# Rounded GELU values of a gated feed-forward block: a second GELU of ScalarE out of PSUM in place of VectorE copies of the first

## The chip, the cores and the metric

The kernel runs on one core of one Trainium2 chip. The metric is the device time of one execution in microseconds (us). Before the change it is 815.6 us, the median of three runs (814.63 to 817.16).

## The reference

A network of two layers is applied to 4 sequences of 1024 tokens of width 128. Each layer is an attention-like mixer and a feed-forward block, each with a residual sum and a layer norm behind it. The change lies in the last feed-forward block, the gated one, with its hidden width of 512:

```python
h = jax.nn.silu(_tlin(x, w1_w, w1_s)) * _tlin(x, w2_w, w2_s)
h = jax.nn.gelu(_tlin(h, h1_w, h1_s), approximate=False)
h = jax.nn.gelu(_tlin(h, h2_w, h2_s), approximate=False)
return _tlin(h, w3_w, w3_s)          # _tlin(x, w, s) = einsum('bsi,oi->bso', x, w) * s
```

The other three parts are a delta-rule attention over chunks of 32 tokens, a mixture of 8 experts (the two best count for each token; all eight are computed here), and a linear recurrence over time (LRU).

## The kernel before

The tokens go through in 8 tiles of 512 columns (4 sequences by 128 tokens), with the features on the partitions. Every large product is made of three float32r products, high by low, low by high and high by high (`mm3`), so each activation is wanted as a high part rounded to float32r and a low part, the difference of the value and its high part.

A software pipeline runs four tiles at a time. Its order is written out by hand and is the same on every engine (`schedule`). Two stages alternate. `dense(m, a, f)` runs the eight experts of tile m, with the delta rule of tile a between them, and at its start the output product of the gated block of tile f. `tails(f, m, a, l)` runs the gated block of tile f (f from 0 to 6), with the recurrence and norms of tile m and the end of attention, router and gates of tile a between its products. Tiles f = 2 to 4 are turns of a hardware loop, f = 0, 1, 5 and 6 are written out. `drain(6, 7)` does the last tile's gated block alone.

The order of `tails` on TensorE is: the gate and up products `glu(f, 0..3)`; `hidden(f, 0, O_H1)` (output blocks 0 and 1 of the first inner layer, into banks 4 and 5); the attention product and `lru_gates(m)`; `hidden(f, 2, O_H1)` (blocks 2 and 3, banks 6 and 7); the second inner layer's blocks 0 and 1 over input chunks 0 and 1; `mean_product`, `router`; the same blocks over input chunks 2 and 3; `var_product`; blocks 2 and 3; `gate_turn(a)`; and then, at the end of the stage, a wait for all four GELUs of the second layer (semaphore `h2_act`), since the next stage writes the banks that they read. In `tails(6, 7, None, 5)` the wait is left out and the drain has its own. TensorE runs its queue in order, so what stands behind that wait is the whole next `dense`.

A block of an inner layer goes through three engines: ScalarE applies GELU out of PSUM into `hf[:, o % 2]` (`gelu`, L1171, counted by `h1_act` or `h2_act`); VectorE copies that into the float32r tile `fbh` (first layer) or `fah` (second) (`hi`, L1888; L1954 in the drain; counted by `h1_hi`, `h2_hi`); GpSimd, called POOL in the profile, subtracts the two into `fbl` or `fal` (L1396, L1404; counted by `fb_ready`, `f2_ready`). The products wait for the last of these. On ScalarE the order of the stage is: four SiLU, norms, `gelu1(0)`, `gelu1(1)`, `lru_tanh` (L1036, L1038), decay and root of the recurrence, attention norm, `gelu1(2)`, `gelu1(3)`, the square of norm 3 (L1001), `gelu2(0)`, `gelu2(1)`, `gate_tanh` (L1057), the logarithm and exponential of norm 3 (table load L1240), `gelu2(2)`, `gelu2(3)`. GELU has its own table, so it is loaded before the first GELU of a group (ACT_TABLE_LOAD at L1171). In the experts a high part comes already from a second GELU of ScalarE (L1139, L1145).

Of the kernel before, what the change touches and what calls it, by code (L numbers as in the profile page):

```python
# [10 lines left out]
ACT = mybir.ActivationFunctionType  # L11
# [15 lines left out]
FC = FF // 128  # L27
# [20 lines left out]
def build(nc, io):  # L48
    ctx = ExitStack()
    with ctx:  # L50
# [25 lines left out]
        vec = sb("vec", [128, N_VEC])  # L76
# [142 lines left out]
        def after(name, n):  # L219

            return S[name], n + CREDIT.get(name, 0)
# [242 lines left out]
        def _(pe):  # L464
# [330 lines left out]
            def hidden(f, o, base, xh, xl, ready, done, chunks=range(FC)):  # L795

                for c, p in [(c, p) for c in chunks for p in (o, o + 1)]:
                    if o == 0 and p == 0:
                        pe.wait_ge(*after(ready, FC * f + c + 1))
                    if base == O_H2 and c == 0:  # L800
                        pe.wait_ge(S["h1_act"], FC * f + p + 1)
                    w = base + c * FF + p * 128
                    i = mm3(bank[4 + p][:, :], wfh[:, w:w + 128], wfl[:, w:w + 128], xh[:, c, :], xl[:, c, :],
                            start=c == 0, stop=c == FC - 1)
                    if c == FC - 1:
                        i.then_inc(S[done], 1)

            def tails(f, m, a, l, inv=0):
                if f is not None:
                    last = f + 2 if m is not None else NT  # L810
                    if isinstance(f, int) and f == 0:
                        pe.wait_ge(S["ws_lo"], NPIECE)
                    pe.wait_ge(*after("x3_ready", f + 1))
                    pe.wait_ge(*after("gelu_done", 3 * E * last))
                    pe.wait_ge(*after("hi1", E * last))
                    glu(f, 0)
                if f is not None:
                    glu(f, 1)
                if a is not None:
                    head_sums(a)  # L820
                if f is not None:
                    glu(f, 2)
                if m is not None:
                    var_product("2", m, m2, 1)
                if f is not None:
                    glu(f, 3)
                    pe.wait_ge(*after("g_act", FC * f + FC - 1))
                    pe.wait_ge(*after("glu_f", FC * f + FC - 1))
                    hidden(f, 0, O_H1, fah, fal, "fa_ready", "h1_done")
                    pe.wait_ge(*after("glu_f", FC * f + FC))  # L830
                if a is not None:
                    if l is not None:
                        pe.wait_ge(*after("rs4", 2 * l + 1))
                    attention_out(a)
                if m is not None:
                    lru_gates(m)
                if f is not None:
                    hidden(f, 2, O_H1, fah, fal, "fa_ready", "h1_done", range(2))
                if a is not None:
                    attention_var(a)  # L840
                if f is not None:
                    hidden(f, 2, O_H1, fah, fal, "fa_ready", "h1_done", range(2, FC))
                if f is not None:
                    hidden(f, 0, O_H2, fbh, fbl, "fb_ready", "h2_done", range(2))
                if m is not None:
                    pe.wait_ge(S["lru_t"], 2 * m + 2)
                    mean_product("3", m, m1, 0)
                if a is not None:
                    router(a)
                if f is not None:  # L850
                    hidden(f, 0, O_H2, fbh, fbl, "fb_ready", "h2_done", range(2, FC))
                if m is not None:
                    var_product("3", m, m2, 1)
                if f is not None:
                    hidden(f, 2, O_H2, fbh, fbl, "fb_ready", "h2_done")
                if a is not None:
                    gate_turn(a)
                leaving = isinstance(f, int) and f == NT - 2
                if f is not None and not leaving:

                    pe.wait_ge(S["h2_act"], FC * f + FC)
                if m is not None and not leaving:

                    pe.wait_ge(*after("d3", m + 1))
                    pe.wait_ge(*after("rs3", 2 * m + 1))

            def drain(l, f):
# [10 lines left out]
                    return mm(bank[2][:, :], wh, xl, start=False, stop=True)  # L878

                pe.wait_ge(*after("x3_ready", f + 1))  # L880
                pe.wait_ge(S["h2_act"], FC * l + 2)
                glu(f, 0)
                output_part(l, 0)
                output_part(l, 1)
                pe.wait_ge(S["h2_act"], FC * l + FC)
                glu(f, 1)
                output_part(l, 2)
                output_part(l, 3).then_inc(S["w3_done"], 1)
# [7 lines left out]
                hidden(f, 2, O_H1, fah, fal, "fa_ready", "h1_done")  # L896
                hidden(f, 0, O_H2, fbh, fbl, "fb_ready", "h2_done")
                for p in (2, 3):
                    pe.wait_ge(S["h1_act"], FC * f + p + 1)
                    for c in range(FC):  # L900
                        w = O_H2 + c * FF + p * 128
                        i = mm3(bank[4 + p][:, :], wfh[:, w:w + 128], wfl[:, w:w + 128], fbh[:, c, :], fbl[:, c, :],
                                start=c == 0, stop=c == FC - 1)
                    i.then_inc(S["h2_done"], 1)
# [13 lines left out]
        def _(act):  # L918
# [246 lines left out]
                A.activation(gb[:, c % 2, :], bank[gate_bank(c)][:, :], ACT.Silu,  # L1165
                             scale=vec[:, V_S1 + c:V_S1 + c + 1]).then_inc(S["g_act"], 1)

            def gelu(f, o, done, acted, v, free, n):
                act.wait_ge(S[done], FC * f + o + 1 + (1 if done in START else 0))
                act.wait_ge(*after(free, n))  # L1170
                A.activation(hf[:, o % 2, :], bank[4 + o][:, :], ACT.Gelu, scale=vec[:, v + o:v + o + 1])\  # L1171
                    .then_inc(S[acted], 1)

            def gelu1(f, o):
                if o < 2:
                    gelu(f, o, "h1_done", "h1_act", V_HS1, "fa_ready", FC * f + 3 + o)
                else:
                    gelu(f, o, "h1_done", "h1_act", V_HS1, "fb_ready", FC * f + o - 1)

            def gelu2(f, o):  # L1180
                if o < 2:
                    gelu(f, o, "h2_done", "h2_act", V_HS2, "fb_ready", FC * f + 3 + o)
                else:
                    gelu(f, o, "h2_done", "h2_act", V_HS2, "f2_ready", FC * f + o - 1)

            def tails(f, m, a, l, inv=0):
                F_, M_, A_, L_ = f is not None, m is not None, a is not None, l is not None
# [237 lines left out]
        def _(dve):  # L1425
# [442 lines left out]
            def tails(f, m, a, l, inv=0):  # L1868
# [13 lines left out]
                    dve.wait_ge(*after("glu_f", k + 1))  # L1882
                    V.tensor_copy(fah[:, c, :], hf[:, c % 2, :]).then_inc(S["glu_hi"], 1)  # L1883

                def hi(o, acted, done, dst, used, n):
                    dve.wait_ge(S[acted], FC * f + o + 1)
                    dve.wait_ge(*after(used, n))
                    V.tensor_copy(dst[:, o, :], hf[:, o % 2, :]).then_inc(S[done], 1)  # L1888

                def hi1(o):  # L1890
                    if F_:
                        hi(o, "h1_act", "h1_hi", fbh, "h2_done", FC * f)

                def hi2(o):
                    if F_:
                        hi(o, "h2_act", "h2_hi", fah, "h1_done", FC * f + FC)

                if F_:
                    glu(0)
                    glu(1)  # L1900
# [5 lines left out]
                    scale("2", m, m1, m3, x2).then_inc(S["x2"], 1)  # L1906
                if L_:
                    scale("4", l, f1, f3, f1).then_inc(S["x4"], 1)
                hi1(0)
                hi1(1)  # L1910
                if M_:
                    lru_input(m)
                    lru_scan(m)
                if A_:
                    attention_sum(a)
                hi1(2)
                if A_:
                    attention_high(a)
                hi1(3)
                if M_:  # L1920
                    centre("3", m, m1, 0)
                if A_:
                    attention_low(a)
                    top_two(a)
                hi2(0)
                hi2(1)
                if isinstance(m, int) and m == NT - 1:
                    scale("3", m, m1, m3, x1).then_inc(S["x3_hi"], 1)
                    dve.wait_ge(S["x3_hi"], 2 * m + 1)
# [2 lines left out]
                    tt(x3l[:, :], x1[:, :], f32(x3h[:, :]), ALU.subtract).then_inc(S["x3_ready"], 1)  # L1932
                if A_:
                    gate_weights(a)
                hi2(2)
                hi2(3)
                if A_:
                    gate_rows(a)

            def drain(l, f):  # L1940
# [8 lines left out]
                    stt(hf[:, c % 2, :], bank[up_bank(c)][:, :], vec[:, V_S2 + c:V_S2 + c + 1],  # L1949
                        gb[:, c % 2, :], ALU.mult, ALU.mult).then_inc(S["glu_f"], 1)  # L1950

                def high(acted, n, done, dst, o):
                    dve.wait_ge(*after(acted, n) if acted == "glu_f" else (S[acted], n))
                    V.tensor_copy(dst[:, o, :], hf[:, o % 2, :]).then_inc(S[done], 1)  # L1954

                product(0)
                dve.wait_ge(*after("w3_done", l + 1))
                dve.wait_ge(*after("out_stored", 16 * l))
                tt(f1[:, :], bank[2][:, :], x3[:, :], ALU.add).then_inc(S["d4"], 1)
                high("glu_f", FC * f + 1, "glu_hi", fah, 0)  # L1960
                for c in range(1, FC):
                    product(c)
                    high("glu_f", FC * f + c + 1, "glu_hi", fah, c)
                scale("4", l, f1, f3, f1).then_inc(S["x4"], 1)
                for o in range(FC):
                    dve.wait_ge(*after("h2_done", FC * f))
                    high("h1_act", FC * f + o + 1, "h1_hi", fbh, o)
                dve.wait_ge(*after("h1_done", FC * f + FC))
                for o in range(FC):
                    high("h2_act", FC * f + o + 1, "h2_hi", fah, o)  # L1970
                dve.wait_ge(S["h2_hi"], FC * f + FC)
                tt(fal[:, FC - 1, :], hf[:, 1, :], f32(fah[:, FC - 1, :]), ALU.subtract).then_inc(S["f2_last"], 1)
                halves = [slice(g * W // 2, (g + 1) * W // 2) for g in range(2)]
# [80 lines left out]
```

## Time and profile before

| | |
|---|---|
| median of three runs | 815.6 us (814.63 to 817.16) |
| the profiled execution, its own time | 813.3 us |
| its span, first to last instruction | 811.3 us |
| granted TensorE clock, mean of the span | 0.962 |
| TensorE (PE) busy | 756.6 us, 93% |
| VectorE (DVE) busy | 576.8 us, 71% |
| ScalarE (ACT) busy | 498.2 us, 61% |
| GpSimd (POOL) busy | 490.3 us, 60% |

Times in the rows are in us from the start of the span, unless marked ns. Rows of a timeline give start, duration, engine, line, operation, output<-input, shape and count; in brackets the idle time of the engine just before and what ended it. Rows that stand for more than one instruction give the time from the first's start to the last's end. Stages: the first `tails` (f = 0) runs from about 278 to 316.7, the turn with f = 3 from 515.4 to 554.8, `tails(6, 7, None, 5)` from 735.7 to 769.8, the drain from there.

### The profile page before, as it was taken

What the parts mean: (1) busy time and instruction counts of PE and PEld (TensorE: products, weight loads), DVE (VectorE), ACT (ScalarE), POOL (GpSimd) and SP (SyncE); (2) the same over time, 40 slices, a digit from 0 to 9 for tenths busy, and PEclk for the clock granted to TensorE, in tenths of its full rate; (3) what the DMA queues carried; (4) which work ended last, traced back from release to release, by engine and by line L of the source; (5) the groups of instructions that cost most, each with busy time, mean ns of one, the idle gap of its engine ahead of it and who ended that gap; (6) DMA issues with size and microseconds to landing.
All of it is one profiled execution on the core that took longest, in us unless ns stands there. A gap on an engine that the chain in (4) does not pass through costs nothing.

```text
span 811.3 us, 11355 instructions
## 1 busy us (share of the span) xinstructions
PE 756.6 (93%) x3492; PEld 582.5 (72%) x3492; DVE 576.8 (71%) x1150; ACT 498.2 (61%) x799; POOL 490.3 (60%) x503
## 2 busy tenths in 40 slices
PE   6999997889899799899989999999999999999996
PEld 4777784667587577767777778777877786777775
DVE  4786788697649757786778678777777777676553
ACT  5877644434935485468546854775577467777763
POOL 0069699269968666787676357534744474286353
PEclk9999898789969899999999999999999999999998
DMA  4134526323131401122013211300130120021000
GB/s 137 50 113 133 164 77 184 107 80 89 42 97 48 127 16 28 40 71 72 28 40 113 57 27 53 103 26 27 63 92 26 36 63 19 1 78 40 1 14 13
DMA packets 47820, 52.68 MB, mean 65 GB/s; under 512 B 2784, under 2 KB 32224, under 8 KB 47776
## 3 DMA queue, kind: packets, MB, share of 16 engines
q1 hardware_dynamic: 47776, 52.13, 22.0%
q8 instruction: 23, 0.38, 0.2%
q14 instruction: 21, 0.17, 0.1%
HBM read 38.62 MB, written 13.50 MB: 64 GB/s over the span
## 4 chain that ended last, share of the span: by engine, by line
PE 70%; DVE 12%; POOL 8%; issue 5%; ACT 3%; DMA 1%; DVEq 0%; SPq 0%; ACTq 0%; POOLq 0%
PE bank L466 70%; POOL fbl L1353 3%; POOL acc L1361 2%; DVE sexp L1622 1%; DVE spread L1614 1%; POOL tmp L1294 1%; POOL tpm L1297 1%; DVE m L1671 1%; DVE x L1605 1%; DVE fbl L1821 1%; DMA xs<-in_xh 1%; POOL texp L1321 1%; DVE yg L1632 1%; DVE x3h L1838 1%; DVE pk L1454 1%
## 5 line engine op out<-in xcount | busy, mean ns | idle before, releaser
L1353 POOL TENSOR_TENSOR fbl<-hf,fbh 128x512 fp32r<-128x512 f32 x64 | 90.0, 1406 | 47.7 <-ACT fbh L1145 47.6
L1133 ACT ACTIVATE hf<-bank 128x512 f32<-128x512 f32 x64 | 38.3, 598 | 117.1 <-PE bank L466 97.0
L1294 POOL TENSOR_TENSOR tmp<-apm,tpm 128x31 f32<-128x31 f32 (+15 forms) x124 | 72.9, 588 | 44.4 <-DVE apm L1486 36.5
L1821 DVE TENSOR_TENSOR fbl<-hf,fbh 128x512 fp32r<-128x512 f32 x64 | 68.7, 1073 | 38.1 <-ACT fbh L1139 38.1
L1297 POOL TENSOR_TENSOR tpm<-tpm,tmp 128x31 f32<-128x31 f32 (+15 forms) x124 | 77.0, 621 | 9.7
L1361 POOL TENSOR_TENSOR acc<-acc,yg 128x512 f32<-128x512 f32 x48 | 69.7, 1453 | 20.8 <-DVE yg L1632 20.8
L1396 POOL TENSOR_TENSOR fbl<-hf,fbh 128x512 fp32r<-128x512 f32 x28 | 37.0, 1324 | 72.6 <-DVE fbh L1888 72.6
L466 PE MATMUL bank<-fal,wfh 128*128 128x512 f32 x160 | 67.7, 423 | 0.0
L466 PE MATMUL bank<-fbl,wmh 128*128 128x512 f32 x128 | 60.0, 469 | 8.1 <-POOL fbl L1353 5.0
L466 PE MATMUL bank<-fah,wfh 128*128 128x512 f32 x160 | 62.5, 390 | 0.0
L466 PE MATMUL bank<-fah,wfl 128*128 128x512 f32 x160 | 62.3, 389 | 0.0
L1171 ACT ACTIVATE hf<-bank,vec 128x512 f32<-128x512 f32 x64 | 42.4, 686 | 27.5 <-PE bank L466 27.2
L1384 POOL TENSOR_TENSOR fal<-hf,fah 128x512 fp32r<-128x512 f32 x28 | 36.1, 1290 | 36.0 <-DVE fah L1883 36.0
L466 PE MATMUL bank<-fbl,wfh 128*128 128x512 f32 x128 | 54.2, 423 | 1.5 <-POOL fbl L1396 1.4
L1404 POOL TENSOR_TENSOR fal<-hf,fah 128x512 fp32r<-128x512 f32 x28 | 36.4, 1309 | 30.0 <-DVE fah L1888 30.0
L466 PE MATMUL bank<-x1l,wmh 128*128 128x512 f32 x128 | 54.3, 424 | 0.0
L1632 DVE TENSOR_TENSOR yg<-bank,gb 128x512 f32<-128x512 f32 x64 | 43.9, 686 | 11.8 <-PE bank L466 10.6
L466 PE MATMUL bank<-fbh,wmh 128*128 128x512 f32 x128 | 51.4, 401 | 0.0
L466 PE MATMUL bank<-fbh,wml 128*128 128x512 f32 x128 | 51.0, 398 | 0.0
L466 PE MATMUL bank<-x1h,wmh 128*128 128x512 f32 x128 | 50.8, 397 | 0.0
L466 PE MATMUL bank<-x1h,wml 128*128 128x512 f32 x128 | 50.7, 396 | 0.0
L466 PE MATMUL bank<-fbh,wfh 128*128 128x512 f32 x128 | 50.0, 391 | 0.0
(241 smaller groups left out, 2153.2 us busy)
## 6 DMA issues: line engine op xcount, KB each, us to landing
gb<-gt SPq DMA_DIRECT2D x64, 256.0 KB, 3.2
pk<-pack SPq DMA_DIRECT2D x7, 1280.0 KB, 7.1
pack<-pk SPq DMA_DIRECT2D x5, 1280.0 KB, 6.9
ws<-in_wf SPq DMA_DIRECT2D x11, 256.0 KB, 3.0
pack<-pk SPq DMA_DIRECT2D x4, 640.0 KB, 3.8
xs<-in_xh SPq DMA_DIRECT2D x8, 262.0 KB, 2.8
xt<-in_xh SPq DMA_DIRECT2D x8, 262.0 KB, 2.9
ws<-in_wm SPq DMA_DIRECT2D x8, 256.0 KB, 3.7
```

Of the source, the lines that this page charges most:

```text
L466: return P.matmul(out, lhsT, rhs, start=start, stop=stop, skip_group_check=skip)
L1133: A.activation(hf[:, 0, :], bank[4][:, :], ACT.Gelu).then_inc(S["gelu_done"], 1)
L1171: A.activation(hf[:, o % 2, :], bank[4 + o][:, :], ACT.Gelu, scale=vec[:, v + o:v + o + 1])\
L1294: G.tensor_tensor(m, a, r, ALU.mult).then_inc(S["t_mul"], 1)
L1297: G.tensor_tensor(o, o, m, ALU.subtract).then_inc(S["t_step"], 1)
L1353: G.tensor_tensor(fbl[:, sl, :], hf[:, 1, :], f32(fbh[:, sh, :]), ALU.subtract)\
L1361: G.tensor_tensor(acc[:, :], (x1 if e == 1 else acc)[:, :], yg[:, (e - 1) % 2, :], ALU.add)\
L1384: G.tensor_tensor(fal[:, c, :], hf[:, c % 2, :], f32(fah[:, c, :]), ALU.subtract)\
L1396: G.tensor_tensor(fbl[:, o, :], hf[:, o % 2, :], f32(fbh[:, o, :]), ALU.subtract)\
L1404: G.tensor_tensor(fal[:, o, :], hf[:, o % 2, :], f32(fah[:, o, :]), ALU.subtract)\
L1632: tt(yg[:, e % 2, :], bank[6][:, :], gb[:, e % 2, :], ALU.mult).then_inc(S["yg_ready"], 1)
L1821: tt(fbl[:, sl, :], hf[:, 0, :], f32(fbh[:, sh, :]), ALU.subtract).then_inc(S["lo0"], 1)
```

## The change

Each GELU of both inner layers is done twice by ScalarE from the same PSUM bank, once into `hf` and once, rounded, into `fbh` or `fah`. The 28 + 28 + 8 copies of VectorE are gone (4 more copies at L1954 belong to the gate product and stay). `h1_hi` and `h2_hi` are counted by ScalarE. TensorE's waits that guard the banks against being overwritten look at `h1_hi` and `h2_hi` (the second read) in place of `h1_act` and `h2_act`. The two waits that VectorE had before overwriting `fbh` and `fah` move to ScalarE.

```diff
@@ TensorE: hidden, end of tails, drain (each of the waits)
-                        pe.wait_ge(S["h1_act"], FC * f + p + 1)
+                        pe.wait_ge(S["h1_hi"], FC * f + p + 1)
...
-                    pe.wait_ge(S["h2_act"], FC * f + FC)
+                    pe.wait_ge(S["h2_hi"], FC * f + FC)
@@ ScalarE
-            def gelu(f, o, done, acted, v, free, n):
-                act.wait_ge(S[done], FC * f + o + 1 + (1 if done in START else 0))
+            def gelu(f, o, done, acted, v, free, n, high, rounded):
+                act.wait_ge(*after(done, FC * f + o + 1))
                 act.wait_ge(*after(free, n))
                 A.activation(hf[:, o % 2, :], bank[4 + o][:, :], ACT.Gelu, scale=vec[:, v + o:v + o + 1])\
                     .then_inc(S[acted], 1)
+                A.activation(high[:, o, :], bank[4 + o][:, :], ACT.Gelu, scale=vec[:, v + o:v + o + 1])\
+                    .then_inc(S[rounded], 1)
 
             def gelu1(f, o):
...
+                if o == 0:
+                    act.wait_ge(*after("h2_done", FC * f))
+                free, n = ("fa_ready", FC * f + 3 + o) if o < 2 else ("fb_ready", FC * f + o - 1)
+                gelu(f, o, "h1_done", "h1_act", V_HS1, free, n, fbh, "h1_hi")
 
             def gelu2(f, o):
...
+                if o == 0:
+                    act.wait_ge(*after("h1_done", FC * f + FC))
+                free, n = ("fb_ready", FC * f + 3 + o) if o < 2 else ("f2_ready", FC * f + o - 1)
+                gelu(f, o, "h2_done", "h2_act", V_HS2, free, n, fah, "h2_hi")
@@ VectorE: tails
-                def hi(o, acted, done, dst, used, n):
-                    dve.wait_ge(S[acted], FC * f + o + 1)
-                    dve.wait_ge(*after(used, n))
-                    V.tensor_copy(dst[:, o, :], hf[:, o % 2, :]).then_inc(S[done], 1)
...
-                hi1(0)
-                hi1(1)
...
-                hi2(2)
-                hi2(3)
@@ VectorE: drain
-                for o in range(FC):
-                    dve.wait_ge(*after("h2_done", FC * f))
-                    high("h1_act", FC * f + o + 1, "h1_hi", fbh, o)
-                dve.wait_ge(*after("h1_done", FC * f + FC))
-                for o in range(FC):
-                    high("h2_act", FC * f + o + 1, "h2_hi", fah, o)
+                dve.wait_ge(S["h2_act"], FC * f + FC)
```

## Rows read from the trace of the kernel before

**Rows 1.** The page, its first part: busy time and share of the span.

```profile
PE 756.6 (93%) x3492; PEld 582.5 (72%) x3492; DVE 576.8 (71%) x1150; ACT 498.2 (61%) x799; POOL 490.3 (60%) x503
```

**Rows 2.** Busy time by stretch: length, PE, PEld, DVE, ACT, POOL, granted clock, DMA.

```profile
524.20:554.80 30.60, 30.41 (x127) 22.03 (x126) 21.50 (x49) 23.60 (x33) 13.65 (x11) 1.00 0.12 33
```

**Rows 3.** Waits of TensorE, 280 to 780: us in total, times, longest.

```profile
PE bank L466 <- DVE a L1624: 4.9, 5, 1.0
PE bank L466 <- POOL fbl L1353: 3.6, 3, 1.6
PE bank L466 <- POOL fbl L1396: 1.4, 3, 0.6
```

**Rows 4.** Timeline of ScalarE, second half of the stage with f = 3.

```profile
529.84 1.26 ACT L1171 ACTIVATE hf<-bank,vec 128x512 f32<-128x512 f32 x2
532.48 0.60 ACT L1036 ACTIVATE m<-bank 128x512 f32<-128x512 f32 x1 [1.38 <-PE bank L466]
...
540.94 1.27 ACT L1171 ACTIVATE hf<-bank,vec 128x512 f32<-128x512 f32 x2
...
546.66 1.38 ACT L1171 ACTIVATE hf<-bank,vec 128x512 f32<-128x512 f32 x2 [1.17 <-PE bank L466]
547.93 0.20 ACT L1057 ACTIVATE gw<-gw 128x4 f32<-128x4 f32 x1
...
550.82 1.28 ACT L1171 ACT_TABLE_LOAD   x1
553.01 1.37 ACT L1171 ACTIVATE hf<-bank,vec 128x512 f32<-128x512 f32 x2 [0.92 <-PE bank L466]
```

**Rows 5.** Timeline of TensorE, the same stage.

```profile
545.03 0.40 PE L466 MATMUL bank<-fbh,wfl 128*128 128x512 f32 x1
545.26 0.40 PE L466 MATMUL bank<-fbh,wfh 128*128 128x512 f32 x1
545.66 0.49 PE L466 MATMUL bank<-fbl,wfh 128*128 128x512 f32 x1
...
553.59 1.04 PE L466 MATMUL bank<-cst,gate 128*8 128x128 f32 x8
554.81 1.08 PE L466 MATMUL bank<-pk,texp 128*128 128x64 f32 x8 [0.18 <-issue]
```

**Rows 6.** Timeline of GpSimd, the same stage: low parts of blocks 2 and 3.

```profile
542.57 1.37 POOL L1396 TENSOR_TENSOR fbl<-hf,fbh 128x512 fp32r<-128x512 f32 x1 [8.60 <-DVE fbh L1888]
544.31 1.30 POOL L1396 TENSOR_TENSOR fbl<-hf,fbh 128x512 fp32r<-128x512 f32 x1 [0.36 <-DVE fbh L1888]
```

**Rows 7.** Timeline of VectorE, the same stage: a copy, and the gate rows.

```profile
542.74 1.49 DVE L1888 CAST fbh<-hf 128x512 fp32r<-128x512 f32 x1
...
555.71 0.67 DVE L1740 COPY gtT<-bank 8x512 f32<-8x512 f32 x1
```

**Rows 8.** Timeline of TensorE, the first stage (f = 0).

```profile
306.18 0.50 PE L466 MATMUL bank<-fbl,wfh 128*128 128x512 f32 x1 [0.41 <-POOL fbl L1396]
...
316.76 1.10 PE L466 MATMUL bank<-pk,texp 128*128 128x64 f32 x8
```

**Rows 9.** Timeline of ScalarE, the first stage (f = 0).

```profile
308.85 1.39 ACT L1171 ACTIVATE hf<-bank,vec 128x512 f32<-128x512 f32 x2 [1.18 <-PE bank L466]
...
315.22 1.37 ACT L1171 ACTIVATE hf<-bank,vec 128x512 f32<-128x512 f32 x2 [0.92 <-PE bank L466]
```

**Rows 10.** Groups of VectorE by form: count, busy us, mean ns, idle before.

```profile
L1632 DVE TENSOR_TENSOR yg<-bank,gb 128x512 f32<-128x512 f32 x64 | 43.9, 686 | 11.8 <-PE bank L466 10.6 <-issue 0.6
...
L1888 DVE CAST fbh<-hf 128x512 fp32r<-128x512 f32 x28 | 24.5, 880 | 7.6 <-ACT hf L1171 7.3
```

**Rows 11.** Timeline of TensorE, the stage with f = 6 and the drain's start.

```profile
760.55 0.50 PE L466 MATMUL bank<-fbl,wfh 128*128 128x512 f32 x1 [0.60 <-POOL fbl L1396]
...
769.79 0.39 PE L466 MATMUL bank<-x3l,wfh 128*128 128x512 f32 x1
```

**Rows 12.** Timeline of VectorE, the last tile's input to the gated block.

```profile
768.22 0.69 DVE L1932 TENSOR_TENSOR x3l<-x,x3h 128x512 fp32r<-128x512 f32 x1
```

More of the change, by code:

```diff
@@ L880, in drain @@
                 pe.wait_ge(*after("x3_ready", f + 1))
-                pe.wait_ge(S["h2_act"], FC * l + 2)
+                pe.wait_ge(S["h2_hi"], FC * l + 2)
                 glu(f, 0)
@@ L884, in drain @@
                 output_part(l, 1)
-                pe.wait_ge(S["h2_act"], FC * l + FC)
+                pe.wait_ge(S["h2_hi"], FC * l + FC)
                 glu(f, 1)
@@ L898, in drain @@
                 for p in (2, 3):
-                    pe.wait_ge(S["h1_act"], FC * f + p + 1)
+                    pe.wait_ge(S["h1_hi"], FC * f + p + 1)
                     for c in range(FC):
@@ L1172, in gelu @@
                     .then_inc(S[acted], 1)
+                A.activation(high[:, o, :], bank[4 + o][:, :], ACT.Gelu, scale=vec[:, v + o:v + o + 1])\
+                    .then_inc(S[rounded], 1)
             def gelu1(f, o):
[L1175 to L1178, printed above, removed]
+                if o == 0:
+                    act.wait_ge(*after("h2_done", FC * f))
+                free, n = ("fa_ready", FC * f + 3 + o) if o < 2 else ("fb_ready", FC * f + o - 1)
+                gelu(f, o, "h1_done", "h1_act", V_HS1, free, n, fbh, "h1_hi")
             def gelu2(f, o):
[L1181 to L1184, printed above, removed]
+                if o == 0:
+                    act.wait_ge(*after("h1_done", FC * f + FC))
+                free, n = ("fb_ready", FC * f + 3 + o) if o < 2 else ("f2_ready", FC * f + o - 1)
+                gelu(f, o, "h2_done", "h2_act", V_HS2, free, n, fah, "h2_hi")
             def tails(f, m, a, l, inv=0):
@@ L1883, in glu @@
                     V.tensor_copy(fah[:, c, :], hf[:, c % 2, :]).then_inc(S["glu_hi"], 1)
-                def hi(o, acted, done, dst, used, n):
-                    dve.wait_ge(S[acted], FC * f + o + 1)
-                    dve.wait_ge(*after(used, n))
-                    V.tensor_copy(dst[:, o, :], hf[:, o % 2, :]).then_inc(S[done], 1)
[L1890 to L1896, printed above, removed]
                 if F_:
@@ L1915, in tails @@
                     attention_sum(a)
-                hi1(2)
                 if A_:
                     attention_high(a)
-                hi1(3)
                 if M_:
@@ L1924, in tails @@
                     top_two(a)
-                hi2(0)
-                hi2(1)
                 if isinstance(m, int) and m == NT - 1:
@@ L1950, in product, with high @@
                         gb[:, c % 2, :], ALU.mult, ALU.mult).then_inc(S["glu_f"], 1)
-                def high(acted, n, done, dst, o):
-                    dve.wait_ge(*after(acted, n) if acted == "glu_f" else (S[acted], n))
-                    V.tensor_copy(dst[:, o, :], hf[:, o % 2, :]).then_inc(S[done], 1)
+                def high(o):
+                    dve.wait_ge(*after("glu_f", FC * f + o + 1))
+                    V.tensor_copy(fah[:, o, :], hf[:, o % 2, :]).then_inc(S["glu_hi"], 1)
                 product(0)
@@ L1959, in drain @@
                 tt(f1[:, :], bank[2][:, :], x3[:, :], ALU.add).then_inc(S["d4"], 1)
-                high("glu_f", FC * f + 1, "glu_hi", fah, 0)
+                high(0)
                 for c in range(1, FC):
                     product(c)
-                    high("glu_f", FC * f + c + 1, "glu_hi", fah, c)
+                    high(c)
                 scale("4", l, f1, f3, f1).then_inc(S["x4"], 1)
-                for o in range(FC):
-                    dve.wait_ge(*after("h2_done", FC * f))
-                    high("h1_act", FC * f + o + 1, "h1_hi", fbh, o)
-                dve.wait_ge(*after("h1_done", FC * f + FC))
-                for o in range(FC):
-                    high("h2_act", FC * f + o + 1, "h2_hi", fah, o)
+                dve.wait_ge(S["h2_act"], FC * f + FC)
                 dve.wait_ge(S["h2_hi"], FC * f + FC)
```

## The prediction, made before the changed kernel was run

> **What bounds the kernel now.** I read the page's busy shares first: TensorE is busy 93% of the span, and no other engine is above 71% [rows 1]. Next the table by stretch, for the half of each `tails` stage in which the inner layers run: TensorE is busy 30.41 of 30.60 us, at a granted clock of 1.00 [rows 2]. So there is nothing to gain there by making VectorE's 71% smaller; there are only TensorE's few waits, and what the change adds to them. The waits of TensorE over all seven stages are short: 1.4 us for the low parts `fbl` of the inner layer, and 8.5 us of the two longest entries that belong to the expert half [rows 3]. None of them names ScalarE. I then read the timelines of one loop turn (f = 3), engine by engine, to see by how little the waits on ScalarE are met.
>
> **What the copies cost.** The 28 copies into `fbh` take 880 ns in the mean [rows 10], because one that meets a GpSimd subtraction lasts as long as that does (1.49 us) [rows 7]. They hold up two things. GpSimd starts the low part of block 3 0.36 us after that of block 2 ended, and TensorE then starts input chunk 3 at 545.66, where the matmul before it began at 545.26, itself 0.23 us after the one before [rows 5, 6]. At that spacing chunk 3 could have begun at 545.49: 0.17 us lost.
>
> With the change, the rounded value of block 2 is there without VectorE. Two GELUs take 1.26 us where one has 0.69 (the group's mean is 686 ns), so they follow each other by 0.57 us [rows 4]. In the group at 540.94 the four are then: value 2 at 540.94, rounded 2 at 541.51 to 542.20, value 3 at 542.08, rounded 3 at 542.65 to 543.34. The low part of block 2 can run from 542.25 (542.57 before), that of block 3 from about 543.6 to 544.9 (ended at 545.61 before), ahead of the 545.49 at which it is wanted. The gain is the 0.17 us in each of f = 2 to 5, and in f = 0 and 1 the 0.41 us ahead of chunk 2 [rows 8] besides: 6 x 0.17 + 2 x 0.41 = 1.8 us. The bounds are nothing and 2.4 us, with the 0.60 us of f = 6 [rows 11].
>
> **What the second GELUs cost at the end of the stage.** This is the term that decides. Call T the start of `gelu2(0)`, 546.66. The pair took 1.38 us (block 1 is done a little after block 0), four take 3 x 0.57 + 0.69 = 2.40 us, so `gate_tanh`, the norm 3 pair and the GELU table load behind them are 1.02 us later. The table was ready at 550.82 + 1.28 = 552.10 and will be ready at 553.12. `gelu2(2)` began at 553.01, when TensorE had its bank done, after 0.92 us of idle [rows 4]: the cover of 0.92 us is used up and 0.1 us is left over. The last four GELUs run from 553.12 to 555.52, where the last pair ended at 554.38. So the semaphore on which the end of the stage waits comes 1.14 us later.
>
> Is there cover on TensorE's side? Its last work, the eight small products of `gate_turn`, ends at 554.63, and the next stage's first product starts at 554.81 behind 0.18 us of issue [rows 5]. That is 0.43 us after the GELU's end at 554.38. In f = 0 the end is at 316.59 and TensorE goes on at 316.76, 0.17 us after [rows 8, 9]. So TensorE is released almost at the same moment by its own work and by ScalarE. If the 0.43 us are register work of the loop that comes behind the wait, there is no cover, and a GELU that ends 1.14 us later delays TensorE by as much. If that work can be done before the wait, some 0.4 us of it are cover. I take no cover, since in f = 0, which is outside the loop, the lag of 0.17 us looks like a plain release: a stall of 1.15 us in each of the six stages that have the wait, f = 0 to 5. 6 x 1.15 = 6.9 us; the lower bound is 6 x 0.75 = 4.5 us.
>
> A rule of the Trainium skill speaks against the change in the same sense: VectorE: DVE Perf Modes, the section on the errata, gives a ScalarE pass out of PSUM 172 cycles plus one for each column at 1.2 GHz, which is 570 ns for 512 columns, and a VectorE copy inside SBUF in its doubled mode only 58 + 256 cycles at 0.96 GHz. By that figure the sum would be the same, for this trace has the same 0.57 us from start to start [rows 4].
>
> **Who waits behind it.** Behind the wait stands the whole expert half. Its waits are 1.0 us five times for VectorE's part of the delta rule and up to 1.6 us for GpSimd's `fbl` [rows 3], but both chains begin with products of TensorE in that half, so they move with it and absorb nothing. I take the stall whole.
>
> **The other places.** The first pair, at 529.84, has 1.38 us of idle behind it before `lru_tanh` [rows 4]; the two more GELUs take 1.14 of them: nothing, with 0.24 us to spare. The pair at 540.94 has more idle behind it. The copies taken off VectorE bring the gate rows (L1740 at 555.71 [rows 7]) forward by about 1.0 us, since `gate_turn` ended at 554.63; nobody waits for that (below). In f = 6 the end wait is missing, but norm 3 of the last tile is 1.0 us later, so `x3l`, ready at 768.22 + 0.69 = 768.91, comes at about 769.95 [rows 12], and TensorE wants it at 769.79, or 0.3 to 0.6 us before that for the wait it no longer has [rows 11]: what f = 6 gains it loses again, and I take zero, between -0.6 and +0.2 us. In the drain the GELUs wait for TensorE and the rounded values are needed later than they come; nothing.
>
> **The sum.** +6.9 - 1.8 + 0 = +5.1 us. The profiled execution has a span of 811.3 us and a time of 813.3 us; it becomes 818.4 us. Its time is 2.3 us under the median of the runs, so against the median of 815.6 us I say 820.7 us, 0.6% slower. The bounds of the terms give +4.5 - 2.4 = +2.1 us to +6.9 us.
>
> **The rivals.**
> *The stall is absorbed* (the expert half is paced by something else than TensorE). The 8.5 us of waits there [rows 3] would have to be set by a chain that does not begin with TensorE. Then only the 1.8 us remain: 813.8 us, no change, and with the 0.6 us of f = 6 813.2, just faster. Against it: every expert's chain is released by a TensorE product in the rows of the groups, L1632 for 10.6 of its 11.8 us of idle [rows 10]. Chance 0.15 for a half or more of it, of which 0.04 comes out faster.
> *The gate rows pace the expert half* (the one on the other side). If the first weighted product L1632 waited for the gate rows, which go out to memory and back, the 1.0 us by which L1740 is earlier would be gained in six stages, TensorE's stall would be hidden behind that wait, and the time is 815.6 - 6.0 - 1.8 = 807.8 us. It decides only when L1632's idle is ended by a transfer; now none of it is [rows 10]. Chance 0.04.
> *ScalarE becomes the bound.* If the second reading of a bank costs its full 0.69 us and not 0.57, four GELUs take 2.76 us. The 0.24 us to spare before `lru_tanh` are gone and the recurrence is late, and the end of each stage is 0.36 + 0.36 us later: 6 x (1.15 + 0.5) = 9.9, less 1.8: +8.1 us, 823.7 us. For it: the rows have no second GELU with a scale vector on the same bank. Against it: the spacing of pairs on two banks is 0.57 [rows 4]. Chance 0.08.
>
> **How the numbers follow.** Forecast: 0.73. With ScalarE as bound 0.08, absorbed 0.15, gate rows 0.04. What this kernel's measurement can tell from no change is about 0.3%, 2.4 us. Of the forecast 0.04 falls inside that (its lower bound is +2.1 us). So slower is 0.69 + 0.08 = 0.77, the same 0.11 + 0.04 = 0.15, faster 0.04 + 0.04 = 0.08. The likeliest case by itself has 817.7 to 822.5 us. The range of eight in ten leaves the gate rows, most of the absorbed case and the outermost of the ScalarE case outside: 815.8 to 823.2 us.
>
> **What the new profile would show.** TensorE's waits have an entry for ScalarE's second GELU with six times about 1.0 us, just ahead of the product `bank<-pk,texp` (or `x1l,wmh` for f = 5). The entry for L1396 is gone. `gelu2(2)` has no idle before it and begins right after its table load. ScalarE is busy 64 x 0.69 = 44 us more, VectorE has lost the group of 24.5 us [rows 10] and the like one into `fah`, and the idle of ScalarE before `lru_tanh` is 0.2 us. If the first entry is missing or near 0.4 us, the cover was larger than I took it; if it is there and the time is not longer, the expert half absorbed it.

## The result, and the profile after

The changed kernel takes 823.15 us, the kernel before 815.15 us (medians of ten runs each; 812.17 to 824.33 and 807.93 to 817.24). The ratio is 1.0079 with a 95% interval of 1.0045 to 1.0113: slower by 6.4 us, between 3.7 and 9.2. (The two medians themselves are 8.0 us apart.) The prediction said 820.7 us, +5.1 us, with 815.8 to 823.2 us as its range: the median lies 2.5 us above the forecast and only just inside the range. Of all executions behind the ratios in this document one is left out, an execution of `layer1_split_preload` that took 1225.72 us at a granted clock of 0.555.

The profiled executions have spans of 811.3 and 818.7 us, 7.4 us apart. Not all of that is the change's. The first work that it touches is the GELUs of the stage f = 0. TensorE's `lru_gates` product of that stage does not yet wait for any of them, and it already starts 2.30 us later. The kernel before:

```profile
292.95 1.88 PE L466 MATMUL bank<-x,wsm 128*128 128x512 f32 x4
```

and the changed kernel:

```profile
295.25 1.88 PE L466 MATMUL bank<-x,wsm 128*128 128x512 f32 x4
```

What lies ahead of it is the ramp, where the two executions were granted different clocks. Busy time by stretch for 120 to 160 us (PE, PEld, DVE, ACT, POOL, then the granted clock and DMA), before and after:

```profile
120.00:160.00 40.00, 31.28 (x142) 22.97 (x141) 28.62 (x70) 18.36 (x33) 25.30 (x38) 0.79 0.51 141
```

```profile
120.00:160.00 40.00, 33.51 (x129) 25.10 (x129) 24.60 (x63) 16.36 (x29) 24.37 (x37) 0.66 0.48 133
```

So every profile below is read by its *changed part*: from the start of that `lru_gates` product to the end of the span. It is 811.3 - 292.95 = 518.35 us before and 818.7 - 295.25 = 523.45 us after, +5.10 us.

The page of the changed kernel, busy time and share of the span [rows 1]:

```profile
PE 757.8 (93%) x3492; PEld 584.1 (71%) x3492; DVE 533.2 (65%) x1086; ACT 531.5 (65%) x863; POOL 488.6 (60%) x503
```

VectorE lost 44 us and ScalarE gained 33 us (and not 64 x 0.69 = 44 us, since consecutive GELUs overlap). TensorE's waits between 278 and 790 us, in total, times, longest [rows 3]:

```profile
PE bank L466 <- ACT fah L1173: 7.5, 6, 1.4
PE bank L466 <- DVE a L1626: 4.9, 5, 1.0
PE bank L466 <- POOL fbl L1355: 3.7, 3, 1.6
...
PE bank L466 <- DVE m L1679: 1.5, 1, 1.5
```

The first entry is new and is the end of the stage, six times. The entry for the inner layer's low parts (L1396 before) is gone. The last one is new too, and it was not forecast. The other two are those of before to 0.1 us: the expert half did not absorb anything.

ScalarE in the stage with f = 3, the loop turn of [rows 4]:

```profile
532.98 1.28 ACT L1171 ACT_TABLE_LOAD   x1 [0.68 <-issue]
534.28 0.69 ACT L1171 ACTIVATE hf<-bank,vec 128x512 f32<-128x512 f32 x1
534.86 0.68 ACT L1173 ACTIVATE fbh<-bank,vec 128x512 fp32r<-128x512 f32 x1
...
550.03 0.69 ACT L1171 ACTIVATE hf<-bank,vec 128x512 f32<-128x512 f32 x1 [1.67 <-PE bank L466]
...
555.23 1.28 ACT L1171 ACT_TABLE_LOAD   x1
556.52 0.69 ACT L1171 ACTIVATE hf<-bank,vec 128x512 f32<-128x512 f32 x1
...
558.25 0.70 ACT L1173 ACTIVATE fah<-bank,vec 128x512 fp32r<-128x512 f32 x1
```

`gelu2(2)` now begins right behind its table load, with no idle. The last GELU ends at 558.25 + 0.70 = 558.95, that is 8.92 us after `gelu2(0)` began; before it was 7.72. The 0.68 us ahead of the first table load are new. TensorE in the same stage [rows 5]:

```profile
548.85 0.40 PE L466 MATMUL bank<-fbh,wfh 128*128 128x512 f32 x1
549.09 0.39 PE L466 MATMUL bank<-fbl,wfh 128*128 128x512 f32 x1
549.32 0.40 PE L466 MATMUL bank<-fbh,wfl 128*128 128x512 f32 x1
...
556.89 1.04 PE L466 MATMUL bank<-cst,gate 128*8 128x128 f32 x8
559.37 0.85 PE L466 MATMUL bank<-pk,texp 128*128 128x64 f32 x6 [1.44 <-ACT fah L1173]
```

Input chunk 3 (549.09) follows the product before it by 0.24 us, without a wait. Behind `gate_turn` there are 1.44 us of waiting, where there were 0.18.

From the starts of `gate_turn` and of the product behind it in every stage, counted from the first `lru_gates` product, the +5.10 us come apart as follows (before, then after, then the difference):

```
                                  f=0           f=1           f=2           f=3           f=4           f=5        sum
to the start of gate_turn   22.84 22.12   80.01 79.20   78.25 77.73   76.38 75.90   76.38 75.90   76.29 75.82
                                -0.72         -0.81         -0.52         -0.48         -0.48         -0.47      -3.48
gate_turn to next product    0.97  2.10    0.97  2.11    1.22  2.48    1.22  2.48    1.22  2.48    0.97  2.11
                                +1.13         +1.14         +1.26         +1.26         +1.26         +1.14      +7.19
behind that: last expert half, f = 6, drain: 101.63, 103.02                                                     +1.39
```

### The profile page after: what moved, and what is told of

Same layout as the page of the kernel before. It is cut to its first block, busy times and chain, and to the rows that moved or that the text cites. A ratio compares the mean times of both kernels' runs of the same rounds, so it can differ in the third digit from the quotient of the medians.

```text
span 818.7 us, 11295 instructions
## 1 busy us (share of the span) xinstructions
PE 757.8 (93%) x3492; PEld 584.1 (71%) x3492; DVE 533.2 (65%) x1086; ACT 531.5 (65%) x863; POOL 488.6 (60%) x503
## 4 chain that ended last, share of the span: by engine, by line
PE 62%; DVE 11%; ACT 11%; POOL 8%; issue 7%; DMA 1%; DVEq 0%; SPq 0%; ACTq 0%; POOLq 0%
PE bank L466 62%; POOL fbl L1355 3%; POOL acc L1363 2%; ACT fah L1173 2%; ACT hf L1171 2%; DVE spread L1616 1%; DVE sexp L1624 1%; ACT L1242 1%; POOL tmp L1296 1%; POOL tpm L1299 1%; DVE fbl L1823 1%; DVE m L1673 1%; ACT L1171 1%; DVE x L1607 1%; DMA xs<-in_xh 1%
## 5 line engine op out<-in xcount | busy, mean ns | idle before, releaser
L1171 ACT ACTIVATE hf<-bank,vec 128x512 f32<-128x512 f32 x64 | 44.0, 688 | 17.9 <-PE bank L466 17.7
```

## The experiments

In each, *changed part* is the quantity above, of one profile. Some profiles hold stretches in the changed part in which TensorE ran at half clock for some 3 us (last section); their cost is read off by comparison of that stage with the same stage of the changed kernel or of a like run, and a second number leaves it out. Ratios are to the kernel before on the same chips, with their 95% intervals.

```
kernel                  changed part   less half-clock stretches   against before    ratio of the times
before                     518.35             518.35                      0
changed                    523.45             523.45                  +5.1          1.0079 [1.0045, 1.0113]
split_wait                 516.87             515.6                   -2.7          1.0002 [0.9973, 1.0031]
preload                    523.21             521.6                   +3.3          1.0025 [0.9992, 1.0058]
split_preload              513.77             513.8                   -4.6          0.9949 [0.9912, 0.9985]
split_preload_2            515.66             513.8                   -4.6          0.9961 [0.9923, 0.9999]
layer1_only                515.96             516.0                   -2.4          0.9982 [0.9940, 1.0024]
layer2_only                528.82             526.8                   +8.5          1.0118 [1.0061, 1.0176]
layer1_split_preload       513.39             513.4                   -5.0          0.9952 [0.9920, 0.9984]
before_split               518.84             517.7                   -0.7          0.9971 [0.9938, 1.0004]
before_waits               519.40             519.4                   +1.1          0.9995 [0.9958, 1.0032]
extra_gelu                 528.09             525.3                   +6.9          not timed against before
```

**split_wait.** The wait at the end of the stage is cut in two. Blocks 0 and 1 (banks 4 and 5) are guarded where they were, blocks 2 and 3 ahead of the output product, the next to write one of their banks.

```diff
@@ TensorE, end of tails
-                    pe.wait_ge(S["h2_hi"], FC * f + FC)
+                    pe.wait_ge(S["h2_hi"], FC * f + 2)
@@ TensorE, output_product(f)
+                pe.wait_ge(S["h2_hi"], FC * f + FC)
                 for c in range(FC):
```

> The changed kernel with the wait at the end of the stage cut in two: at the end of the stage TensorE waits for the rounded GELUs of blocks 0 and 1 alone, and for those of blocks 2 and 3 ahead of the output product, which writes bank 6. Theory A (the stall behind h2_hi is what makes the changed kernel slower, and the expert half absorbs none of it): the six waits of 1.1 to 1.4 us for the second GELU, 7.5 us in all in the changed kernel, go to nothing, and the part of the span from the first stage's lru_gates product on is 7 us shorter than in the changed kernel, about 2 us shorter than before. Rival B (the expert half would have waited anyway, or waits now ahead of the output product): the six waits reappear there and the kernel stays within 1 us of the changed one.

TensorE's waits between 278 and 795 us:

```profile
PE bank L466 <- DVE a L1627: 4.9, 5, 1.0
PE bank L466 <- POOL fbl L1356: 3.6, 3, 1.6
...
PE bank L466 <- DVE m L1680: 1.5, 1, 1.5
```

The entry for ScalarE is gone and has not come back elsewhere. The end of the loop turn, TensorE and then ScalarE:

```profile
555.10 1.04 PE L466 MATMUL bank<-cst,gate 128*8 128x128 f32 x8
556.07 1.10 PE L466 MATMUL bank<-pk,texp 128*128 128x64 f32 x8
```

```profile
556.46 0.70 ACT L1174 ACTIVATE fah<-bank,vec 128x512 fp32r<-128x512 f32 x1
```

The next half's first product starts 0.97 us after the start of `gate_turn`, 1.1 us before the last rounded GELU ends at 557.16; the output product, which needs it, only comes at 558.46. The changed part is 7.8 us shorter than in the changed kernel, for 7.5 us of waits taken away: theory A. The whole time is that of the kernel before, and its interval (0.9973 to 1.0031) lies below that of the changed kernel (1.0045 to 1.0113); the 2.7 us against before that the profile shows do not stand out of an interval of 0.3% each way.

**preload.** The GELU table is asked for explicitly, ahead of the waits of each group of GELUs (`gelu1(0)`, `gelu1(2)`, `gelu2(2)`, and in the drain).

```diff
                 if F_:
+                    A.preload_act_table_set(GELU)
                     gelu1(f, 0)
                     gelu1(f, 1)
...
```

> The changed kernel with the GELU table asked for ahead of the waits of each group of GELUs. Theory A (in the changed kernel the load at L1171 stands behind the wait for the first inner layer's product, 0.68 us late in the loop and 1.62 us late in the stage f = 6, and that makes the recurrence late, 1.49 us of TensorE waiting for m at f = 6): the load has no idle before it, TensorE's wait for m at f = 6 is gone or under 0.3 us, and the kernel is 1.3 us shorter than the changed one, all of it in f = 6. Rival B (the recurrence is late because of the two more GELUs ahead of it): the wait for m stays at 1 us or more. Rival C: the load costs nothing that TensorE sees and nothing moves.

Stage f = 6, the table load and the first GELU of the changed kernel:

```profile
754.53 1.28 ACT L1171 ACT_TABLE_LOAD   x1 [1.62 <-issue]
755.83 0.69 ACT L1171 ACTIVATE hf<-bank,vec 128x512 f32<-128x512 f32 x1
```

and of this one:

```profile
747.01 1.28 ACT L1217 ACT_TABLE_LOAD   x1
748.63 0.69 ACT L1171 ACTIVATE hf<-bank,vec 128x512 f32<-128x512 f32 x1 [0.34 <-issue]
```

The load no longer has idle before it; what little is left stands before the GELU itself. TensorE's product that waits for the recurrence, `mean_product`, in the changed kernel:

```profile
766.56 1.10 PE L466 MATMUL bank<-m,cst 128*128 128x512 f32 x2 [1.49 <-DVE m L1679]
```

and in this one:

```profile
759.36 1.10 PE L466 MATMUL bank<-m,cst 128*128 128x512 f32 x2 [0.21 <-DVE m L1683]
```

1.49 us have become 0.21: theory A, against rival B, which wanted 1 us or more. The second GELUs are not free there, though: the 0.21 us are theirs, for the load is early again. Outside f = 6 the saving was expected to be zero, and that was wrong; the changed part without its half-clock stretch is 1.8 us shorter, of which the part behind f = 5 (last expert half, f = 6, drain) accounts for 1.28 (101.74 against 103.02), f = 0 for 0.37 (`gate_turn` at 21.75 instead of 22.12) and f = 1 for 0.29 (78.91 instead of 79.20). The time by itself, ratio 1.0025, only says that it is not clearly faster or slower than before.

**before_waits.** The kernel before, with nothing but the change's two added waits on ScalarE, which are met long before.

```diff
             def gelu1(f, o):
+                if o == 0:
+                    act.wait_ge(*after("h2_done", FC * f))
```

and the same for `gelu2` with `h1_done`.

> The kernel before, with the change's two added waits on ScalarE ahead of gelu1(0) and gelu2(0) and nothing else; both are met long before. Theory A (the added wait moves the table load behind the wait for the product): ScalarE is idle ahead of the load at L1171 for some 0.7 us in a loop turn and more in f = 6, as in the changed kernel, and the recurrence of f = 6 is late by 0.5 to 1 us. Rival B (the load stands late for another reason, the shape of the changed helper): no idle ahead of the load, nothing moves.

```profile
744.31 1.28 ACT L1171 ACT_TABLE_LOAD   x1 [1.63 <-issue]
```

ScalarE is idle 1.63 us ahead of the load at f = 6, and 0.68 us in the loop turn, to 0.01 us as in the changed kernel; all groups at L1171 together have 7.0 us of such idle, eight times, in both. In the kernel before, the load of the loop turn had no idle ahead of it and the first GELU followed at 529.84:

```profile
528.55 1.28 ACT L1171 ACT_TABLE_LOAD   x1
```

TensorE waits 0.8 us for `m` (in f = 0, 1 and 6, 0.3 at the longest) and the changed part is 1.1 us longer than before: 0.3 us in each of f = 0 and 1, and 0.54 us behind f = 5. Theory A: a wait that is always met costs this, by where it puts the table load. In f = 6 that is 0.5 us, and not the 1.4 us of the changed kernel: the late load alone does not make the whole of it.

**layer1_only, layer2_only.** The change in one inner layer alone: the other layer's rounded values come from VectorE's copies, and the bank waits of the second layer (respectively the first) look at `h2_act` (`h1_act`) as before. The diff is that of `layer1_only`; `layer2_only` has "h2_hi" there.

```diff
+                if rounded == "h1_hi":
+                    A.activation(high[:, o, :], bank[4 + o][:, :], ACT.Gelu, scale=vec[:, v + o:v + o + 1])\
+                        .then_inc(S[rounded], 1)
...
```

> The change in the first inner layer alone: second GELUs for fbh, VectorE copies for fah, the bank waits for the second layer on h2_act as before. Theory A: the gains of the changed kernel before gate_turn stay (0.5 us in a loop turn, 0.7 to 0.8 us in f = 0 and 1), there is no stall at the end of the stage, f = 6 keeps its 1.4 us; from the first lru_gates product on about 2 us shorter than before. Rival B (the gain comes from VectorE as a whole): gains of half that.

> The change in the second inner layer alone: second GELUs for fah, VectorE copies for fbh. Theory A: the end of the stage has the stall of the changed kernel (six waits for ScalarE, some 7 us), while the gains ahead of gate_turn are gone (0 to 0.1 us in a loop turn where the changed kernel has 0.5); from the first lru_gates product on 6 to 8 us longer than before. Rival B (both layers' GELUs together make the stall): less than half of it.

With the first layer alone the changed part is 2.4 us shorter than before; TensorE has no wait for ScalarE at the end of a stage and still 1.5 us for `m` at f = 6. The way to `gate_turn` is as in the changed kernel (22.10, 79.17, 77.80 and 75.92 us in f = 0 to 3, where that has 22.12, 79.20, 77.73 and 75.90), and its gain over all six stages is 3.5 us in both: theory A, not the half of rival B. The times (ratio 0.9982) do not tell this kernel from the one before. With the second layer alone TensorE's waits between 278 and 795 us begin:

```profile
PE bank L466 <- ACT fah L1174: 7.4, 6, 1.4
...
PE bank L466 <- POOL fbl L1399: 1.4, 3, 0.6
```

All of the stall and none of the gain, and 8.5 us longer than before: the two halves of the change have opposite signs, by the place of their GELUs in the stage. This kernel, timed in four executions, also has the highest ratio, 1.0118. It exceeds the upper end of what was expected (8 us) by 0.5 us: 7.1 us are the stall, 0.5 us lie in f = 0 and 1 as in `before_waits`, and 1.0 us behind f = 5, where `before_waits` has 0.54 (0.1 us is gained elsewhere). The other 0.5 us there stand at the start of the drain, 0.4 of them by its second product `bank<-x3l,wfh`, and belong to the second layer's GELUs.

**before_split.** The kernel before with the wait cut in two.

> The kernel before with the wait at the end of the stage cut in two, copies of VectorE as they were. Theory A (before the change TensorE and ScalarE released the next stage at nearly the same moment, so the wait cost next to nothing): from the first lru_gates product on at most 0.18 us a loop turn shorter, 0.5 us in all, and the run is the same as before. Rival B (the wait already cost the loop's 0.4 us, as register work behind it): 1.5 to 2 us shorter.

`gate_turn` to the next product is 0.97 us in the loop turns instead of 1.22, three times 0.25: some 0.7 us in all, between the two theories and nearer to A, whose 0.18 us a turn it exceeds. The wait cost the kernel before a quarter of a microsecond in a loop turn and nothing in the written-out stages. Its time, ratio 0.9971 with 1.0004 at the upper end, does not decide.

**split_preload, split_preload_2.** Both edits in the changed kernel.

> Both edits together. If the two causes are independent, the part of the span from the first stage's lru_gates product on is 7 + 1.3 = 8.3 us shorter than in the changed kernel and about 3.3 us shorter than before (0.4% faster than before). If the end stall hides behind the same delay as the table load, less than the sum, some 7 us.

> The same kernel as split_preload once more, to narrow its time against the kernel before: 0.5% faster than before (ratio 0.994 to 0.996), with an interval that leaves out 1.

The changed part is 9.7 us shorter than in the changed kernel and 4.6 us shorter than before, where 8.3 and 3.3 were expected. The two single edits measured 7.8 and 1.8 us, which add up to 9.6: the two effects are independent. In the second run, less its half-clock stretch, the changed part is the same to 0.1 us. Both timings have 1 outside the interval, the second only just (0.9999, at a ratio of 0.9961 where 0.994 to 0.996 was expected): this version is faster than the kernel before by about 0.4 to 0.5%, and its intervals lie wholly below that of the changed kernel.

**layer1_split_preload.** The same with the second inner layer by VectorE copies.

> The first inner layer by second GELUs, the second by VectorE copies, with the wait cut in two and the GELU table asked for early. Against the version with both layers and both edits: the second layer's rounded GELUs no longer lie on ScalarE, so the low parts of blocks 2 and 3 come from VectorE; if the second layer's change is worth nothing by itself the two are within 1 us, some 4 us shorter than before from the first lru_gates product on. If it is worth something, this one is 1 to 2 us longer.

513.4 against 513.8 us, and ratios of 0.9952 and 0.9949: the second layer's second GELUs are worth nothing even where their stall is removed. By the profile they still cost 0.4 us, all of it behind f = 5 (101.79 against 101.41), at the start of the drain. So the gain comes from the first layer's second GELUs and the two edits. What both edits are worth without any second GELU was not run; the cut wait alone is worth 0.7 us there (`before_split`).

**extra_gelu.** The changed kernel with one more GELU of 128 columns, between the two of the last block.

```diff
+                if acted == "h2_act" and o == 3:
+                    act.wait_ge(*after("extra", f))
+                    A.activation(dump[:, :], bank[4 + o][:, 0:128], ACT.Gelu, scale=vec[:, v + o:v + o + 1])\
+                        .then_inc(S["extra"], 1)
...
```

> The changed kernel with one more GELU, of 128 columns into a spare tile, between the two GELUs of the last block of the second inner layer; it works on nothing that is used. An estimate from the profile's GELUs: 0.2 to 0.4 us more on ScalarE in each stage, x in the profile. Theory A (a delay at the end of the stage goes through to the end of the kernel one to one): the six waits for ScalarE are each x longer and the part of the span from the first lru_gates product on is 6 times x longer than in the changed kernel, 1.2 to 2.4 us. Rival B (the expert half absorbs part): clearly less than 6 times x.

ScalarE, the end of the loop turn, and TensorE's waits:

```profile
557.67 0.38 ACT L1176 ACTIVATE dump<-bank,vec 128x128 f32<-128x128 f32 x1
557.92 0.70 ACT L1178 ACTIVATE fah<-bank,vec 128x512 fp32r<-128x512 f32 x1
```

```profile
PE bank L467 <- ACT fah L1178: 9.1, 6, 1.7
```

The GELU pushes the next by 0.25 us, the six waits grow by 9.1 - 7.5 = 1.6 us (0.27 each), and the changed part grows by 4.6 us, of which 2.8 lie in two half-clock stretches and 1.8 remain: 1.6 from `gate_turn` to the next product in the six stages, 0.3 behind f = 5. So the delay goes through one to one. One of the two stretches stands behind a lengthened stall; that the extra GELU set it off is not shown, since `preload` has one without it. This kernel was run once.

## Why the prediction was right, step by step

**The stall at the end of the stage**, forecast at six times 1.15 = 6.9 us, is 7.19 us. The mechanism is as it was put: the 0.92 us of cover of `gelu2(2)` are used up by the two more GELUs ahead of the table load (it starts right behind the load), the four GELUs take 2.43 us (2.40 were forecast), and nothing absorbs it. `split_wait` takes away the wait and the time with it, `layer2_only` has it alone, `extra_gelu` lengthens it in proportion. The doubtful point, whether the loop's 0.43 us behind the GELU could be cover, was decided rightly: TensorE goes on at 559.37, 0.42 us after 558.95, so the lag stands behind the wait. What it consists of is not shown; `before_split` shows that it cost the kernel before 0.25 us in a loop turn. The reason given, that the 0.17 us of f = 0 are a plain release, was not right. In f = 0 the changed kernel goes on 0.05 us after its last GELU's end (319.42, 319.47), so that is the plain release; before, TensorE went on 0.97 us behind the start of `gate_turn`, as in `before_split`, by its own work. Outside the loop there was 0.12 us of cover, which is why the stall there is 1.13 us and in the loop 1.26 us.

**The gain ahead of `gate_turn`**, forecast at 1.8 us, is 3.5 us. The step that was mis-sized is the 0.17 us for a wait. A wait costs more than its idle: before, the matmul behind it began 0.40 us after its predecessor and the next one 0.33 us after that, where 0.23 is usual (545.26, 545.66, 545.99), so the short wait cost 0.27 us and not 0.17. The prediction also put the place ahead of chunk 2 at nothing in a loop turn. The low part of block 2 ended at 542.57 + 1.37 = 543.94 [rows 6] and chunk 2 began at 544.00, 12.63 us behind `lru_gates`; in the changed kernel it begins 12.47 us behind it (547.62), and its second product 0.19 us earlier than before. The two places make the 0.48 us of a loop turn but for 0.02. In f = 0 and 1 the gain is net of the late table load: with `preload` it is 1.09 us at f = 0 instead of 0.72.

**Stage f = 6**, forecast at zero, is +1.4 us. This is the step that failed, in two places. The prediction let `x3l` be late and the gain of 0.60 us be lost by it, and took the recurrence as unharmed, because 1.38 us of idle before `lru_tanh` would hide the two more GELUs. Those 1.38 us were read in the turn with f = 3. In f = 6 the kernel before had 0.23 us:

```profile
750.12 0.60 ACT L1036 ACTIVATE m<-bank 128x512 f32<-128x512 f32 x1 [0.23 <-PE bank L466]
```

And it took the table load to stay where it was. The added wait on ScalarE, which the prediction did not cost at all, put the load behind the wait for the first layer's product: 0.68 us of idle ahead of it in a loop turn, 1.62 us in f = 6.

The runs show the two parts one by one. Counted from `lru_gates`, `lru_tanh` of f = 6 starts at 1.12 us before, at 2.00 with the late load alone (`before_waits`), at 1.85 with the second GELUs alone (`preload`), and at 3.13 with both. `mean_product`, which waits for the recurrence, starts at 9.92, 10.43, 10.29 and 11.57 in these four. Some 0.36 us of each delay are hidden. So each alone costs TensorE 0.4 to 0.5 us, and both together 1.65 us. The 0.60 us of waiting for `fbl` is gained as was said, and the second layer's GELUs cost some 0.4 us at the start of the drain (the prediction's bound for `x3l` was 0.2): 1.65 - 0.60 + 0.4 is the +1.4 us.

In a loop turn the late load moves `lru_tanh` too, from 1.11 to 1.42 us behind `lru_gates`, so the forecast 0.24 us of idle ahead of it are gone (with `preload` they are there, 0.22 us). `mean_product` does not feel it: it starts at 10.80 us in both kernels.

**The sum** was +5.1 us and the changed part measured +5.10. That is partly luck: the stall was 0.3 us and f = 6 1.4 us worse than said, the gain was 1.7 us larger, and the errors cancel. The interval of the timed difference, 3.7 to 9.2 us, holds the 5.1 us.

**The rivals.** Absorbed: no, the expert half's own waits are unchanged. Gate rows: no, the copy of L1740 comes earlier (1.08 us behind the start of `gate_turn` and not 2.12) and nothing follows. ScalarE at its full 0.69 us a pass: no, the second reading of one bank follows the first by 0.57 to 0.58 us (534.28, 534.86). The Trainium skill (VectorE: DVE Perf Modes, the errata section) counts 172 cycles plus one for each column at 1.2 GHz for a ScalarE pass out of PSUM, 570 ns for 512 columns; the trace agrees from start to start, while one pass lasts 0.69 us in it.

## What to carry to other kernels

Ask of each instruction moved to an idle-looking engine which wait ends last behind it: by the profiles the same edit gained 2.4 us in the first layer, whose values were awaited by products, and lost in the second, where the engine's end released the next stage. Read the idle time that is to cover a delay in every written-out stage, and not in one loop turn: 1.38 us in the turn were 0.23 us in the last stage. A wait that guards several buffers at the end of a stage can be cut up and put where each buffer is next written; that took away 7.8 us in the changed kernel, and 0.7 us in the kernel before, where the wait was hardly felt. And a wait added "for order" on ScalarE is not free even when it is always met: look where the table load goes, and ask for the table ahead of the waits.

## What the hardware showed that was not expected

A wait of TensorE of 1.4 us or more was in some executions followed by a stretch at half clock. In the profile of `preload`, behind the stall at the end of a stage, by stretch (PE, PEld, DVE, ACT, POOL, granted clock):

```profile
470.00:474.50 4.50, 3.06 (x22) 2.26 (x21) 0.68 (x1) 2.98 (x5) 2.48 (x2) 1.00 0.02 4
475.60:478.40 2.80, 2.80 (x8) 2.21 (x7) 0.69 (x1) 1.91 (x4) 0.62 (x1) 0.50 0.57 181
478.60:483.00 4.40, 4.04 (x23) 3.19 (x22) 1.74 (x6) 1.04 (x3) 0.46 (x1) 1.00 0.00 0
```

The granted clock is 0.50, 1.2 GHz in place of 2.4 GHz, and eight products of 512 columns follow each other by 0.43 us in place of 0.23: 1.6 us lost. `extra_gelu` has the same behind a stall of 1.73 us:

```profile
561.10:564.30 3.20, 3.20 (x9) 2.54 (x8) 0.69 (x1) 2.03 (x4) 1.07 (x1) 0.50 0.44 154
```

In `split_wait`, `split_preload_2`, `layer2_only`, `before_split` and once more in `extra_gelu` it stands behind the 1.58 us wait for GpSimd's `fbl` in the expert half ahead of f = 2, and costs 1.2 to 2.0 us. The changed parts of the kernel before and of the changed one have the same waits and no such stretch, so it is no rule that one wait of this length brings it. Behind a longer wait, 3.29 to 3.31 us for `x3l` at the start of stage f = 0, all twelve profiles have it: the granted clock is 0.50 from 276.00 to 281.30 us in the kernel before, where 11 products follow each other by 0.43 us, and from 279.40 to 282.20 us in the changed one, where 5 do. That lies outside the changed part. The stretches may be part of why the timed difference (6.4 us) lies above the 5.1 us of the profile; that is not shown. The clock in the ramp differs too (0.79 against 0.66 in the rows above). The fastest execution of the changed kernel, 812.17 us, had a mean granted clock of 0.974, the three slowest, above 824 us, had 0.956; so a profile has to be compared stage by stage here and not by its span.
